# Softmax row sums: accumulating DMAs and a fourth bank for the maxima in an attention kernel

## The reference

```
xn  = layernorm(x)
q,k,v = xn @ W.T + b                  (16 heads of 32 channels; q is scaled by 1/sqrt(32))
attn  = softmax(q k^T) v              (2048 x 2048 scores per head, 4 x 16 = 64 heads in all)
out   = x + (attn @ out_w.T + out_b) + tanh(xn @ weight @ aux1 @ aux2 + bias)
```

## Time and profile before

| | |
|---|---|
| median of 3 runs | 4560.37 us (4559.83 to 4561.25) |
| profiled execution | 4557.16 us, span 4555.4 us |
| TensorE (PE) busy | 4454.8 us, 98% |
| GpSimd (POOL) busy | 3200.7 us, 70% |
| VectorE (DVE) busy | 2943.1 us, 65% |
| ScalarE (ACT) busy | 2358.1 us, 52% |
| granted TensorE clock, mean | 0.989 |

### The profile page before, as it was taken

The page is one execution under the profiler, slowest core; times in us unless marked ns, Lnnn a source line. Parts: engine busy times, 40 slices in busy tenths (PEclk is TensorE's granted clock), DMA queues, the critical chain, the costliest instruction groups (busy, mean ns, idle before and its releaser), DMA issues.

```text
span 4555.4 us, 81083 instructions
## 1 busy us (share of the span) xinstructions
PE 4454.8 (98%) x23776; PEld 2528.8 (56%) x23776; DVE 2943.1 (65%) x4928; ACT 2358.1 (52%) x4517; POOL 3200.7 (70%) x863
## 2 busy tenths in 40 slices
PE   7999999999999999999999999999999999999999
PEld 5888888554545454545454545445445545455457
DVE  3343433777777777777777777777777777777534
ACT  1222222265666565666665666666666666666631
POOL 0222221488888888888888888888888888888830
PEclk9999999799999999999999999999999999999999
DMA  4444445312222221122222211121222222111157
GB/s 155 159 157 154 166 144 176 77 35 51 45 44 43 44 44 44 43 44 46 45 55 46 46 44 43 44 44 43 44 46 44 49 51 49 44 43 43 47 176 258
DMA packets 288290, 338.44 MB, mean 74 GB/s; under 512 B 169984, under 2 KB 171008, under 8 KB 275584
## 3 DMA queue, kind: packets, MB, share of 16 engines
q1 hardware_dynamic: 286384, 332.48, 26.8%
q10 hardware_dynamic: 1488, 0.79, 0.1%
HBM read 195.30 MB, written 137.36 MB: 73 GB/s over the span
## 4 chain that ended last, share of the span: by engine, by line
PE 74%; ACT 3%; issue 3%; DVE 2%; DMA 0%; POOL 0%; ACTq 0%; DVEq 0%; SPq 0%; POOLq 0%
PE sm_bank L774 22%; PE st_bank L790 21%; PE pv_bank L796 20%; PE sum_bank L796 7%; ACT probs L646 3%; PE sm_bank L191 3%; DVE part_max L715 1%; PE st_bank L191 1%; PE sm_bank L783 0%; POOL pool_sum L613 0%; DVE k_stack L729 0%; ACTq L645 0%; DMA s_sums<-sum_copy 0%; DMA q_stack<-max_row 0%; DVE probs L737 0%
## 5 line engine op out<-in xcount | busy, mean ns | idle before, releaser
L715 DVE TENSOR_REDUCE part_max<-sm_bank 128x1 f32<-128x512 f32 x4096 | 2508.3, 681 | 826.6 <-PE sm_bank L774 822.7
L613 POOL TENSOR_TENSOR pool_sum<-pool_sum,probs 128x2048 f32<-128x2048 f32 x576 | 2639.6, 4583 | 426.9 <-ACT probs L646 405.2
L646 ACT ACTIVATE probs<-st_bank 128x512 f32<-128x512 f32 x4096 | 2080.6, 616 | 1116.4 <-PE st_bank L790 1080.9
L774 PE MATMUL sm_bank<-k_stack,q_stack 96*128 96x512 f32 x4096 | 1732.1, 427 | 35.5 <-issue 16.3
L790 PE MATMUL st_bank<-q_stack,k_stack 97*128 97x512 f32 x4096 | 1613.3, 412 | 28.9 <-ACT probs L646 26.0
L774 PEld LDWEIGHTS sm_bank<-k_stack,q_stack 96*128 96x128 f32 x4096 | 780.8, 191 | 658.8 <-issue 279.7
L796 PE MATMUL pv_bank<-probs,v_head 128*32 128x512 f32 x8192 | 1024.7, 601 | 0.0
L790 PEld LDWEIGHTS st_bank<-q_stack,k_stack 97*128 97x128 f32 x4096 | 774.6, 189 | 405.1 <-ACT probs L646 272.0
L796 PEld LDWEIGHTS pv_bank<-probs,v_head 128*32 128x32 f32 x8192 | 214.1, 109 | 448.0 <-issue 268.9
L613 POOL TENSOR_TENSOR pool_sum<-probs 128x2048 f32<-128x2048 f32 x64 | 293.6, 4588 | 99.5 <-ACT probs L646 99.5
L291 POOL TENSOR_TENSOR y_out<-y_out,x_in 128x512 f32<-128x512 f32 x64 | 82.8, 1293 | 370.1 <-ACT y_out L320 364.2
(11 more groups left out here) (84 smaller groups left out, 2030.8 us busy)
## 6 DMA issues: line engine op xcount, KB each, us to landing
q_stack<-s_q_hi SPq DMA_DIRECT2D x128, 256.0 KB, 4.6
k_stack<-s_k_hi SPq DMA_DIRECT2D x128, 256.0 KB, 6.1
x_in<-in_x SPq DMA_DIRECT2D x16, 1024.0 KB, 7.8
s_q_hi<-qk_hi SPq DMA_DIRECT2D x16, 1024.0 KB, 4.3
s_q_lo<-qk_lo SPq DMA_DIRECT2D x16, 1024.0 KB, 6.4
s_k_hi<-qk_hi SPq DMA_DIRECT2D x16, 1024.0 KB, 4.3
s_k_lo<-qk_lo SPq DMA_DIRECT2D x16, 1024.0 KB, 6.4
s_v<-v_out SPq DMA_DIRECT2D x16, 1024.0 KB, 4.3
```

Of the source, the lines that this page charges most:

```text
L613: nc.gpsimd.tensor_tensor(total[:], one[:], probs[kt % PROBS][:], ALU.add).then_inc(pool_added, 1)
L646: nc.scalar.activation(probs[kt % PROBS][:, q * BLK:(q + 1) * BLK], st_bank[:, st_place(kt * QB + q)], ACT.Exp, scale=SCALE).then_inc(prob ...
L715: nc.vector.tensor_reduce(part_max[:, k:k + 1], sm_bank[:, sm_place(sm_slot(k))], AX.X, ALU.max).then_inc(max_scores_read, 1)
L774: nc.tensor.matmul(sm_bank[:, sm_place(sm_slot(k))], q_st[r][0:ROWS, q * P:(q + 1) * P], k_st[r][0:ROWS, b * BLK:(b + 1) * BLK], start=Tru ...
```

## The change

The row sums of a head are divided anew. Tiles 0, 2, 5, 8, 10 and 13 go to a new tile dma_sum: tile 0 is copied into it by a plain DMA from SP (first_tile), and the five others are added by DMAs with an add, issued by GpSimd (join) after its adds 0, 2, 4, 6 and 7; each join waits until the one before has landed. The ten other tiles are added by GpSimd as before, in nine adds. TensorE no longer spreads any probs tile with ones: add_up spreads dma_sum and pool_sum. SCALE_ADD goes from 6 to 7. The exponentials that reuse a buffer wait for the DMA that has read it.

The maxima have four banks instead of three; the sums share one of them, as a slot of the ring after max unit 39, and the turned maxima have a slot after unit 7. CUT is 6, so that the sums of a head are spread a pair of tiles later, and copied by ScalarE after tile 5. RECIP_UNIT is 56. The alternation of scores and max scores is the same in all tiles (LATE is gone).

SP sends the row of maxima of the head after next behind the ratios and ahead of the store of the context, where it sent it at the start of the next turn of its loop. In the output projection the result tiles and banks are chosen anew.

```diff
-BANKS = 3
+SM_BANKS, ST_BANKS = 4, 3
-TURN_SLOT = 8
-RECIP_UNIT = 48
-CUT = 4
-LATE = 1
-DIRECT = [2, 5, 8, 11, 14]
-POOL_TILES = [kt for kt in range(KT) if kt not in DIRECT]
+TURN_UNIT = 8
+SUM_UNIT = 40
+RECIP_UNIT = 56
+CUT = 6
+DMA_TILES = [0, 2, 5, 8, 10, 13]
+POOL_TILES = [kt for kt in range(KT) if kt not in DMA_TILES]
 POOL_ADDS = len(POOL_TILES) - 1
-SCALE_ADD = 6
+JOINED = (len(DMA_TILES) - 1) * DMA
+JOIN_AFTER = {0: 1, 2: 2, 4: 3, 6: 4, 7: 5}
+SCALE_ADD = 7
+SM_TURN = [*range(TURN_UNIT), "max", *range(TURN_UNIT, SUM_UNIT), "sum", *range(SUM_UNIT, UNITS), None, None]
+
+def sm_place(what):
+    return SM_TURN.index(what) % SM_BANKS
+
+def sm_before(what):
+    slot = SM_TURN.index(what) - SM_BANKS
+    while SM_TURN[slot] is None:
+        slot -= SM_BANKS
+    return SM_TURN[slot], int(slot < 0)
...
+            def first_tile(h, r):
+                sp.wait_ge(probs_ready, PRIME + h * UNITS + QB * (DMA_TILES[0] + 1))
+                sp.dma_start(dma_sum[r % 2][:], probs[DMA_TILES[0] % PROBS][:]).then_inc(first_copied, DMA)
...
             load_row(0, 0)
+            first_tile(0, 0)
+            load_row(1, 1)
             def body(h, r, more, following):
                 if more >= 1:
-                    load_row(following, (r + 1) % GROUP)
+                    first_tile(following, (r + 1) % GROUP)
...
                 spread_ratios(h, r)
+                if more >= 2:
+                    load_row(following + 1, (r + 2) % GROUP)
                 store(h, r)
...
+            def join(h, r, j):
+                if j == 1:
+                    pool.wait_ge(first_copied, PRIME + h * DMA + DMA)
+                    if not (isinstance(h, int) and h == 0):
+                        pool.wait_ge(joined, h * JOINED)
+                else:
+                    pool.wait_ge(joined, h * JOINED + (j - 1) * DMA)
+                pool.sem_inc(join_due, 1)
+                nc.gpsimd.dma_start(dma_sum[r % 2][:], probs[DMA_TILES[j] % PROBS][:],
+                                    accum_op=ALU.add).then_inc(joined, DMA)
...
+            def sum_up(h, r, i):
+                add(h, r, i)
+                if i in JOIN_AFTER:
+                    join(h, r, JOIN_AFTER[i])
...
                         if old in POOL_TILES:
                             act.wait_ge(pool_added, PRIME + h * POOL_ADDS - back * POOL_ADDS + adds_after(old))
+                        elif old == DMA_TILES[0]:
+                            act.wait_ge(first_copied, PRIME + h * DMA + DMA)
+                        elif not (back and isinstance(h, int) and h == 0):
+                            act.wait_ge(joined, h * JOINED - back * JOINED + DMA_TILES.index(old) * DMA)
...
-                pe.wait_ge(max_scores_read, PRIME + s * UNITS + sm_units_before(k))
-                if k == TURN_SLOT + BANKS - 1:
+                old, back = sm_before(k)
+                if old == "max":
                     pe.wait_ge(max_row_ready, s)
+                elif old == "sum":
+                    pe.wait_ge(sums_copied, PRIME + s - 1)
+                else:
+                    pe.wait_ge(max_scores_read, PRIME + s * UNITS - back * UNITS + old + 1)
...
-                last = spread(pv_bank, v_sb[r][:, kt], tile, kt == 0, kt == KT - 1)
-                if kt in DIRECT:
-                    if kt == DIRECT[0]:
-                        pe.wait_ge(sums_copied, PRIME + h)
-                    last = spread(sum_bank, ones[:], tile, kt == DIRECT[0], False)
-                last.then_inc(tile_used, 1)
-
-            def add_partial(h, r):
+                spread(pv_bank, v_sb[r][:, kt], tile, kt == 0, kt == KT - 1).then_inc(tile_used, 1)
+
+            def add_up(h, r, more):
+                if more >= 2:
+                    pe.wait_ge(max_scores_read, PRIME + h * UNITS + 2 * UNITS + sm_before("sum")[0] + 1)
+                pe.wait_ge(joined, h * JOINED + JOINED)
+                spread(sum_bank, ones[:], dma_sum[r % 2], True, False)
                 pe.wait_ge(pool_added, PRIME + h * POOL_ADDS + POOL_ADDS)
                 spread(sum_bank, ones[:], pool_sum[r % 2], False, True).then_inc(sums_ready, 1)
...
                 for q in range(QB):
-                    if kt % 2 and q >= LATE:
-                        scores(h, r, kt, q)
                     if more >= ahead:
                         max_scores(s, (r + ahead) % GROUP, k0 + q)
-                    if kt % 2 == 0 or q < LATE:
-                        scores(h, r, kt, q)
+                    scores(h, r, kt, q)
```

More of the change, by code:

```diff
@@ L38 @@
 AHEAD = 4
-TURN_SLOT = 8
-RECIP_UNIT = 48
-CUT = 4
-LATE = 1
-DIRECT = [2, 5, 8, 11, 14]
-POOL_TILES = [kt for kt in range(KT) if kt not in DIRECT]
+TURN_UNIT = 8
[4 more added lines that the diff above has]
+POOL_TILES = [kt for kt in range(KT) if kt not in DMA_TILES]
 POOL_ADDS = len(POOL_TILES) - 1
-SCALE_ADD = 6
+JOINED = (len(DMA_TILES) - 1) * DMA
+JOIN_AFTER = {0: 1, 2: 2, 4: 3, 6: 4, 7: 5}
+SCALE_ADD = 7
+RESULT_TILES = [9, 11]
 PACK = SEQ // P
[L52 to L66, removed]
+SM_TURN = [*range(TURN_UNIT), "max", *range(TURN_UNIT, SUM_UNIT), "sum", *range(SUM_UNIT, UNITS), None, None]
[6 more added lines that the diff above has]
+    return SM_TURN[slot], int(slot < 0)
 def st_slot(u):
@@ L74, in st_place @@
 def st_place(u):
-    return st_slot(u) % BANKS
+    return st_slot(u) % ST_BANKS
 def st_units_before(u):
     return next(v for v in range(u - 1, u - UNITS, -1) if st_place(v % UNITS) == st_place(u)) + 1
-assert UNITS == 64 and sm_slot(UNITS - 1) == 64 and st_slot(UNITS - 1) == 65
+assert UNITS == 64 and len(SM_TURN) % SM_BANKS == 0 and st_slot(UNITS - 1) == 65
 def adds_after(kt):
@@ L444, in build_attend @@
         pool_sum = [sb(f"pool_sum{s}", [P, SEQ]) for s in range(2)]
+        dma_sum = [sb(f"dma_sum{s}", [P, SEQ]) for s in range(2)]
         ones, ident = sb("ones_att", [P, DH]), sb("ident_att", [P, P])
@@ L451, in build_attend @@
         ctx_out = [sb(f"ctx_out{s}", [P, BLK]) for s in range(2)]
-        st_bank = ps("st_bank", [P, BANKS, BLK])
-        sm_bank = ps("sm_bank", [P, BANKS, BLK])
+        st_bank = ps("st_bank", [P, ST_BANKS, BLK])
+        sm_bank = ps("sm_bank", [P, SM_BANKS, BLK])
         pv_bank = ps("pv_bank", [P, BLK])
-        sum_bank = ps("sum_bank", [P, BLK])
+        sum_bank, turn_bank = sm_bank[:, sm_place("sum")], sm_bank[0:QT, sm_place("max"), 0:P]
         consts_ready, ident_zero = sem("consts_ready"), sem("ident_zero")
@@ L471, in build_attend @@
         ctx_hi, ctx_lo = [tiled(q_st[2]), tiled(q_st[1])], [tiled(k_st[2]), tiled(k_st[1])]
-        res = [tiled(probs[DIRECT[2] % PROBS]), tiled(probs[DIRECT[3] % PROBS])]
-        out_banks = [sm_bank[:, 0], sm_bank[:, 1], sm_bank[:, 2], st_bank[:, 0]]
+        res = [tiled(probs[kt % PROBS]) for kt in RESULT_TILES]
+        out_banks = [sm_bank[:, b] for b in range(SM_BANKS) if b != sm_place("sum")] + [st_bank[:, 0]]
         assert len(out_banks) == JT and BLK == DIM
@@ L504, in _ @@
                 sp.sem_inc(s, PRIME)
+            sp.sem_inc(first_copied, PRIME)
             def load(h, r):
@@ L619, in scale @@
                 nc.gpsimd.tensor_tensor(ctx_out[r % 2][:], pv_copy[r % 2][:], ratio[:], ALU.mult).then_inc(context_ready, 1)
+            def sum_up(h, r, i):
+                add(h, r, i)
+                if i in JOIN_AFTER:
+                    join(h, r, JOIN_AFTER[i])
             for i in range(POOL_ADDS):
-                add(0, 0, i)
+                sum_up(0, 0, i)
             def body(h, r, more, following):
@@ L628, in body @@
                     if more >= 1:
-                        add(following, (r + 1) % GROUP, i)
+                        sum_up(following, (r + 1) % GROUP, i)
             heads(pool, body)
@@ L698, in negate @@
                 dve.wait_ge(turned_ready, s + 1)
-                nc.vector.tensor_scalar(max_row[:], sm_bank[0:QT, sm_place(TURN_SLOT), 0:P], -1.0, None,
+                nc.vector.tensor_scalar(max_row[:], turn_bank, -1.0, None,
                                         ALU.mult).then_inc(max_row_ready, 1)
@@ L708, in maxima @@
                 for k in range(UNITS):
-                    if k == TURN_SLOT and new:
+                    if k == TURN_UNIT and new:
                         negate(s - 1)
@@ L781, in turn_max @@
                 if s_next:
-                    pe.wait_ge(max_scores_read, PRIME + s * UNITS + UNITS + TURN_SLOT - BANKS + 1)
-                nc.tensor.transpose(sm_bank[0:QT, sm_place(TURN_SLOT), 0:P], row_max[:], ident[:]).then_inc(turned_ready, 1)
+                    pe.wait_ge(max_scores_read, PRIME + s * UNITS + UNITS + sm_before("max")[0] + 1)
+                nc.tensor.transpose(turn_bank, row_max[:], ident[:]).then_inc(turned_ready, 1)
             def scores(h, r, kt, q):
@@ L822, in both_scores @@
                     s, ahead, k0 = following + 1, 2, PER_TILE * (kt - KT + AHEAD)
-                if k0 == TURN_SLOT and more >= 1:
+                if k0 == TURN_UNIT and more >= 1:
```

(11 more changed lines are left out.)

10 lines of the change are left out of this document (6 added, 4 removed).

## The result

The changed kernel takes 4740.55 us (median, 4738.93 to 4741.08) against 4560.57 before: the ratio is 1.0394 (95% interval 1.0376 to 1.0412), 180 us slower. The forecast was 4327 with 4265 to 4480, so the sign was wrong too. From the page of the profile: busy times, granted clock in 40 slices, and the chain by engine and line, which answers to the earlier trace rows.

A forecast was written before the change was run, and what follows sets the result against it. TensorE was taken as the bound, GpSimd close behind. Heads falling from 53.72 to 49.9 us save 237 us over 62 heads, less 4 at the end: 4557.2 to 4324, plus 3 for the median, 4327; range 4265 to 4480.

The forecast's parts named there:

- TensorE's own part: TensorE per head: four spreads go, 3.44 us, and score stages give 0.4 us, leaving 49.9 us.
- GpSimd: GpSimd's work per head: nine adds, the scaling and five DMA issues, 47.5 us, under TensorE's 49.9.
- L: Time of one 1 MB accumulating DMA from issue to landing, put at 7.1 us.
- lands at 64.0: Timetable of joins: join 5, issued by 56.9 us after the head's start, lands at 64.0.
- p0: First of a head's eight pairs of key tiles on TensorE; its start is the timetable's zero.
- C: Length of a head; joins' deadlines need at least 49.2 and 49.3 us, just below TensorE's 49.9.
- Rival (4): Join 5 lands beyond 9.3 us, ScalarE waits before next head's tile 5; each further us costs 2 us a head; 11%.
- p2: Third of a head's eight pairs of key tiles on TensorE, forecast to take 8.10 us.
- even: SP's plain copy of tile 0 lands by 15 us, wanted by join 1 at 15.4.
- hiccups: Some 0.8 us per head on average that the head examined lacks; left unchanged by the forecast.
- The row of maxima: SP's row of maxima lands at 48.3 us, wanted at 50.2: no cost, 1.9 us of margin.
- The end: Last head: ScalarE's first split of the output projection waits for GpSimd's scaling, about 4 us lost once (0 to 10).

The follow-up runs named there:

- e8: e3 with three banks shared by maxima and sums instead of four; 4424.8 us, ratio 0.9702.
- e12: e3 with scores and max scores in the old order in odd tiles, four banks kept; 4313.9 us, ratio 0.9457.
- e3: Changed kernel with the five accumulating DMAs of a head moving 16 columns of 2048; 4255.7 us, ratio 0.9332.
- e2: Changed kernel with all seven loads of heads 4 to 59 moving 16 columns (one tile for v); 4427.4 us, ratio 0.9712.
- e7: Changed kernel with the row of maxima sent behind the store and the seven loads, as before the change; 5672.2 us, ratio 1.2434.
- e4: Changed kernel with four joins instead of five: GpSimd adds tile 13, TensorE spreads tile 15 out of probs; 4513.3 us, ratio 0.9904.
- e10: e4 with twelve heads per loop turn and head loads split into q, k and v parts at separate places; 4315.1 us, ratio 0.9464.
- e5: Changed kernel with twelve heads per turn of the loop instead of four; 4672.0 us, ratio 1.0246.
- e6: Kernel before the change with twelve heads per turn of the loop; 4531.2 us, ratio 0.9933.
- e1: Changed kernel with SP issuing the seven head loads right after the sums' load instead of behind the store; 4577.3 us, ratio 1.0046.

## Why the prediction was wrong

**TensorE's own part: right, and undersized.** Four spreads were to take 3.44 us off a head; they took 3.4. From the score stages I took 0.4 us and gave 1.2 as the most; it was 1.6, so an undisturbed head takes 48.7 and not 49.9. I had bounded the gain by the chain's rows of the maxima. e8 and e12 show that without the fourth bank (51.4) or without the plain order (49.9) it is gone, wholly or in the larger part. This alone would have put the time below the forecast: e3, where hardly anybody waits for the joins, takes 4255.7, under the 4265 at which the range begins.

**GpSimd: right in sum, by luck in part.** An issue was put at 1.0 us. It shows as 0.88, and the next add starts 0.61 us after it (2014.12 to 2014.73). The adds, of which the ones behind an issue take 4.88, take 4.75 on the mean instead of 4.58, and the scaling behind an issue 1.56 instead of 1.29. By these, 9 x 4.75 + 1.56 + 5 x 0.61 = 47.4 us per head, against the 47.5 of the sum: the issue was put too high and the adds too low by about as much.

**L: right, where nothing is beside it.** The estimate was 7.1 us; joins 1 to 4 land in 7.0 to 7.4. The Trainium skill (Collectives: The Full Stack, The bandwidth ceiling) says that two source reads halve the rate of an add within a DMA. The trace agrees with that for the moving and not for the whole. With 8 KB a join lands in 2.0 us (e3), so a megabyte adds 5.1 us, 1.8 times the 2.8 that the prediction works out for a plain one; the whole is 7.1, not the 8.6 of twice 4.3.

**The step that failed is "lands at 64.0" of join 5.** Put the head above on the prediction's axis: the next p0 is at 2007.6, which is C = 49.9, so 0 is at 1957.7. Then join 5 was issued at 56.4, against 55.9 in the prediction, and its deadline was at 64.3, against 64.6 (49.9 + 14.7): the timetable was right to half a microsecond. Only the landing was not: at 67.9. I had seen that join 5 meets the loads, and priced it at nothing, with the words that "the loads are past their middle when join 5 starts". They were not. The store ahead of them took SP 4.0 us instead of the 1.94 read from before: over all heads it takes 4.05 in the median with a join in flight (56 heads), 1.91 without (8 heads), and 1.84 in e3. So the loads began only 1.5 us ahead of join 5. Join 5's own packets begin 3.3 us behind its issue, where those of joins 1 to 4 begin at 1.45, and while it is under way SP's queue moves 1.6 MB (medians). Nor did the rows allow the words: by the earlier trace rows the engines are full for 13 us from the store's start, at 50.1 on that axis, so until 63, and join 5 was to be in them from 55.9 to 64.0. The Trainium skill (DMA: Bandwidth & Descriptors, Issuing engines are not separate DMA queues) says that DMAs of all issuing engines run on the same 16 and interleave. The trace agrees, with 11.7 us for join 5 and 7.0 to 7.4 for joins 1 to 4, beside which SP's queue moves at most 0.15 MB (medians).

**Rival (4) is what happened**, with its place and its direction, at 11%: join 5 beyond 9.3 us. Its price does not fit. The price of 2 us a head for each us takes both joins 4 and 5 to be slower, and by it 11.7 us would give 4560 + 62 x 4.8 = 4858. With join 5 alone late, its own timetable gives C = 48.8 + 7.1 + 1.0 + 11.7 - 14.7 = 53.9, no loss to speak of; the heads took 55 and 57. What the price lacked is what a stop of 4 us brings behind it: the four spreads of p2 take 5.4 us in the median (4.4 to 6.2) instead of 3.6, much of it at half the clock, and the plain copy, which I had called "even", comes 7.8 us late to join 1.

**The turn of the loop was a second term put at nothing**, with the hiccups that were left "as they are". Before, the 0.8 us per head are 3.2 us at each turn (56.9 against 53.7). With whole joins and small loads (e2) it is 13 to 18, as the wait behind the branch grew from 2.5 to 6.1 us on ScalarE and from 2.7 to 6.2 on VectorE. They come one after the other: at the turn shown above TensorE stops 5.3 us for ScalarE at 2040.8 and 5.1 us for VectorE at 2066.2, and each time it goes on at half the clock.

The sum, from runs: small joins and small turns 4255.7 - 4560.6 = -305; whole joins without loads, e2 less e3, +172, nearly all of it at the turns; the loads beside whole joins, changed kernel less e2, +313. Together +180; the steps are taken in this order, and with small joins the loads cost the heads between turns nothing (48.7 in e3). The forecast had -233 and nothing for the other two.

**The row of maxima: right.** No wait, and e7 shows what it would be otherwise.

**The end.** From the last turn of the maxima to the end of the span it is 4737.1 - 4476.3 = 260.8 us, where it was 253.4: 7.4 more, within the 0 to 10 given for it. This takes in the output projection, which was changed too. So it is not shown that the scaling of the last head is the cause.

**What stays open.** e2 and e3 show that the wait at the turn follows the joins' bytes, and the packets show that the instruction queues' packets come late there. Why they come late in the engines is inferred: that they stand behind the joins' packets. No run takes the loss of the 55 and 57 us heads apart into the late copy and the half clock.

## What to carry to other kernels

A DMA that takes over work from an engine has a time that depends on its neighbours: lay all DMAs of a period on one time axis with those of the other queues, and take the landing beside traffic, not alone, for each that has a deadline within a few microseconds. What paid here was to leave the one with the tightest deadline to a compute engine (e4), and to cut bulk loads, which have a head of slack, in pieces and put them between the others (e10). At a loop's turn bulk DMAs in flight can stop the compute engines; longer bodies make that rarer (e5, e6).

## What the runs showed of the hardware

A 1 MB accumulating DMA between two SBUF tiles lands in 7.0 to 7.4 us (medians of joins 1 to 4), one of 8 KB in 2.0 (e3). Beside 1.75 MB of loads the first takes 11.7 (at most 14.2) and the second 7.6. GpSimd's next instruction starts 0.6 us after its issue. SP's issue of a plain 1 MB copy is 0.5 us in the median where the loads are not ahead of it (e1, e10), 6.6 behind seven loads, 8.8 in e5. SP's four issues of a store take 1.9 us, and 4.05 with an accumulating DMA in flight. ScalarE's first instruction behind a loop's branch comes 2.5 us after it in the kernel before and 6.1 with whole joins. TensorE, stopped for 3.9 us from 2022.5, had a granted clock of 0.5, its level of 1.2 GHz, from 2025.1 to 2031.9; at the turn of the kernel before it stops for 1.1 us and the clock stays at full.
